# Language-model block: earlier slots for tile 0's layer norm and for the first weight splits

## The reference, cut to what matters

```
h = rms_norm(rms_norm(emb[ids]) @ proj.T)
h = h + attention(layernorm(h)) @ wo      # 32 query heads, 8 key/value heads of 16, causal softmax
h = h + (silu(n @ w_gate.T) * (n @ w_up.T)) @ w_down.T     with n = layernorm(h), 2048 hidden
layernorm(x) = (x - mean(x)) / sqrt(var(x) + 1e-5)
```

## Time and profile before

| | |
|---|---|
| median of three runs | 723.34 us (723.07 to 725.62) |
| profiled execution | 722.81 us, span 721.0 us |
| TensorE busy | 693.3 us (96%) |
| VectorE busy | 414.4 us (57%) |
| ScalarE busy | 334.5 us (46%) |
| GpSimd busy | 295.6 us (41%) |
| mean granted TensorE clock | 0.986 of full |

### The profile page before, as it was taken

The page is one execution under the profiler, slowest core; times in us unless marked ns, Lnnn a source line. Parts: engine busy times, 40 slices in busy tenths (PEclk is TensorE's granted clock), DMA queues, the critical chain, the costliest instruction groups (busy, mean ns, idle before and its releaser), DMA issues.

```text
span 721.0 us, 16350 instructions
## 1 busy us (share of the span) xinstructions
PE 693.3 (96%) x6399; PEld 530.2 (74%) x6399; DVE 414.4 (57%) x1041; ACT 334.5 (46%) x691; POOL 295.6 (41%) x398
## 2 busy tenths in 40 slices
PE   8459989999999999999999999999999999999998
PEld 5359679974898569965997489856996499847873
DVE  7867789885654556554655465555655365543320
ACT  6426368862565226631665046622674066512320
POOL 5020212241365426752565436642665246611220
PEclk9859999999999999999999999999999999999999
DMA  8759410011000110002000210012000300000000
GB/s 319 306 196 401 150 40 2 2 28 63 33 2 1 61 61 2 2 17 97 9 2 2 69 54 3 1 47 76 2 2 1 107 15 2 1 16 15 2 1 29
DMA packets 10459, 40.37 MB, mean 56 GB/s; under 512 B 1808, under 2 KB 2576, under 8 KB 8592
## 3 DMA queue, kind: packets, MB, share of 16 engines
q1 hardware_dynamic: 6912, 25.44, 9.1%
q0 software_dynamic: 3328, 13.11, 5.7%
q10 hardware_dynamic: 144, 0.79, 0.3%
HBM read 29.89 MB, written 9.44 MB: 55 GB/s over the span
## 4 chain that ended last, share of the span: by engine, by line
PE 88%; DVE 8%; ACT 2%; issue 1%; POOL 1%; DVEq 0%; POOLq 0%; ACTq 0%
PE banks L1106 15%; PE banks L1108 15%; PE banks L1107 15%; PE banks L1197 6%; PE banks L1199 6%; PE banks L1198 6%; PE banks L1060 4%; PE banks L1078 3%; PE banks L1049 2%; PE banks L1142 2%; PE banks L1144 2%; PE banks L1143 2%; PE banks L1084 1%; PE banks L1038 1%; PE banks L1085 1%
## 5 line engine op out<-in xcount | busy, mean ns | idle before, releaser
L1108 PE MATMUL banks<-xnT_and_h,ffn_weights 128*128 128x256 f16 x1024 | 279.0, 272 | 0.0
L1106 PE MATMUL banks<-xnT_and_h,ffn_weights 128*128 128x256 f16 x1024 | 278.8, 272 | 0.1
L1107 PE MATMUL banks<-xnT_and_h,ffn_weights 128*128 128x256 f16 x1024 | 278.9, 272 | 0.0
L374 POOL TENSOR_TENSOR gated_split<-gate_work,gated_split 128x256 f16<-128x256 f32 x128 | 86.7, 678 | 260.6 <-ACT gated_split L518 260.6
L378 POOL TENSOR_TENSOR weights_split<-weights,weights_split 128x512 f16<-128x512 f32 x96 | 111.3, 1159 | 0.0
L1106 PEld LDWEIGHTS banks<-xnT_and_h,ffn_weights 128*128 128x128 f16 x1024 | 101.0, 99 | 11.9 <-DVE xnT_and_h L878 0.6
L1108 PEld LDWEIGHTS banks<-xnT_and_h,ffn_weights 128*128 128x128 f16 x1024 | 100.0, 98 | 11.8
L1107 PEld LDWEIGHTS banks<-xnT_and_h,ffn_weights 128*128 128x128 f16 x1024 | 99.9, 98 | 11.2
L506 ACT ACTIVATE gate_work<-banks,scales 128x256 f32<-128x256 f32 x128 | 60.7, 474 | 99.8 <-PE banks L1108 99.7
L828 DVE SCALAR_TENSOR_TENSOR weights<-weights,counts_T 128x512 f32<-128x512 f32 x128 | 87.8, 686 | 11.6 <-ACT weights L514 11.5
L514 ACT ACTIVATE weights<-banks,scales 128x512 f32<-128x512 f32 x128 | 87.3, 682 | 14.5 <-PE banks L1060 14.5
(11 more groups left out here) (232 smaller groups left out, 1063.9 us busy)
## 6 DMA issues: line engine op xcount, KB each, us to landing
ffn_weights<-in_ffn_w SPq DMA_DIRECT2D x12, 1024.0 KB, 11.2
out_rows_dram<-ffn_weights SPq DMA_DIRECT2D x16, 256.0 KB, 2.0
xnT_and_h<-in_wqkv SPq DMA_DIRECT2D x1, 1536.0 KB, 8.6
local_table<-gated_split SPq DMA_DIRECT2D x2, 640.0 KB, 4.4
local_table<-xnT_and_h SPq DMA_DIRECT2D x2, 640.0 KB, 6.0
gated_split<-in_projT SPq DMA_DIRECT2D x4, 256.0 KB, 4.0
ffn_weights<-in_wo SPq DMA_DIRECT2D x1, 1024.0 KB, 10.6
token_table<-weights_split ACTq DMA_DIRECT2D x1, 768.0 KB, 5.2
```

Of the source, the lines that this page charges most:

```text
L374: g.tensor_tensor(gtl[:, j, :], g2[j % 2], gth[:, j, :], ALU.subtract).then_inc(gt_lo, 1)
L1106: t.matmul(o, wh, xTh[m % 2][:, c, :], start=c == 0, stop=False)
L1107: t.matmul(o, wh, xTl[m % 2][:, c, :], start=False, stop=False)
L1108: last = t.matmul(o, wl, xTh[m % 2][:, c, :], start=False, stop=c == DC - 1)
```

## The change

Only three tables change; no instruction is added or removed. In phase 0, steps of tile 0 go to earlier slots, as do the fetch for tile 2 and the splits of the first chunks. Four chunks were split by the end of phase 0, and then there are five. In phase 1 each chunk from 5 on is split one slot earlier than before. Steps of tile 1 stay where they are.

```diff
-FIRST_SLOTS = dict(yt=(11, 18), wo=(13, 19), ln=(16, 20), rs=(17, 20), xhat=(19, 20), xn=(20, 21), xl=(21, 21), fetch=(17, 20), m=(22, 3))
+FIRST_SLOTS = dict(yt=(11, 18), wo=(13, 19), ln=(14, 20), rs=(16, 20), xhat=(17, 20), xn=(19, 21), xl=(20, 21), fetch=(15, 20), m=(22, 3))
-HI_FIRST = {16: 0, 17: 1, 20: 2, 21: 3}
-LOW_FIRST = {19: (0,), 21: (1,), 22: (2,), 23: (3,)}
-HI_NEXT = {i - 4: i for i in range(4, NCH)}
+HI_FIRST = {16: 0, 17: 1, 18: 2, 20: 3, 21: 4}
+LOW_FIRST = {17: (0,), 19: (1,), 20: (2,), 22: (3,), 23: (4,)}
+HI_NEXT = {i - 5: i for i in range(5, NCH)}
```

## The result

Ten executions of each kernel: 726.16 us median after the change (725.14 to 729.36) against 724.59 before (723.07 to 725.62); the ratio is 1.0031, with a 95% interval of 1.002 to 1.0041. By the ratio that is 2.2 us more, by the medians 1.6. The profiled execution has a span of 723.4 us (721.0 before) and a time of 725.14.

The account below looks back on a forecast made before the run. Tile 1's chain was taken to set the gate/up start, with TensorE's own work behind it. Parts 1 and 2 gave 1.2 us, sum and fillers 0.7 to 0.8: +2.0 on 723.34, so 725.3, range 723.9 to 727.3.

Parts of the forecast that it names:

- The rest is TensorE's own work: Behind about 97.7 us TensorE runs its own order, so the end moves exactly as the first gate/up start does.
- Part 1: Slots 14 to 17: ln(0) and rs(0) move ahead of pair 7 on VectorE; its end comes 1.13 us later.
- Part 2: Slot 17: xhat(0) and chunk 0's split stand ahead of slot 18's subtraction, which starts 1.23 us later.
- the other branch of that working: The subtraction starting by ScalarE's copy, at 83.97; the forecast had VectorE's queue end last, at 84.35.
- Part 3: Slot 20: chunk 2's split delays the diagonal; sum and fillers add 0.7 to 0.8 us, gate/up +2.0 in all.
- Part 4 and 5: ScalarE's splits and chunks five ahead: priced 0, bounds 0 and +0.3; earlier fetches on GpSimd: nothing.
- Sum: Whole kernel: +2.0 us on the median 723.34 of the runs gives 725.3.
- likeliest range: Whole kernel, the likeliest case's own range: +1.3 to +2.6 us, 724.6 to 725.9.
- The clock rival: Clock falls on the thin stretch ahead of gate/up, 90.7 to 94 us: 727.3 us; chance 0.10.
- The price of 2.0: Clock fall's cost at 90.7 to 94 us: upper end of 1.2 to 2.0 us, taken for 727.3.
- the forecast place: The stretch from 90.7 to 94 us, ahead of gate/up, where a clock fall was placed.
- none of them is longer than 1.5 us: Argument against a clock fall: new TensorE idle times are short; the earlier fall came in a stretch without matmuls.

Follow-up runs that it names:

- norm_only: Kernel before with only tile 0's ln and rs moved, to slots 14 and 16; median 725.28 us against 724.36, ratio 1.0015.
- diag_first: Changed kernel with the down gram's diagonal ahead of chunk 2's split in slot 20; median 725.58 us against 724.36 of the kernel before, ratio 1.0015.
- again3: Changed kernel measured again without any edit, in a later group; median 725.99 us, ratio 1.0027 to the kernel before.
- again: Changed kernel measured once more without any edit; median 727.76 us, ratio 1.0051 to the kernel before.
- splits_only: Kernel before with only the three split tables as changed; median 726.28 us against 724.36, ratio 1.0029.
- rs_behind: Kernel before with tile 0's rs in slot 19, chunk 0's split halved, chunks 2, 3 high later, slots 14, 15 fillers removed; 724.73 us against 722.55, ratio 1.0012.

## Why the prediction was right, point by point

- **The rest is TensorE's own work.** Right: the end less the gate/up start is 628.0 us in both kernels, and 628.0 to 628.1 in every variant whose clock was full from gate/up on.
- **Part 1, the ready mark +1.13.** Measured +1.12, on the common scale, with the idle time of "over 1 us" at 1.03.
- **Part 2, chunk 0 ahead of the subtraction, +1.23 in all.** Measured 13.17 - 11.99 = 1.18 at the output product; xhat(1) 1.19. norm_only confirms the other branch of that working: without the split the chain goes by ScalarE's copy, +0.88.
- **Part 3, the diagonal, sum and fillers.** Forecast 0.7 to 0.8, measured 3.53 - 2.68 = 0.85, and 0.80 of it is back in diag_first. The sum waited 0.86 for L745, as said.
- **Part 4 and 5, nothing.** Right as far as the rest of 628.0 us and the unchanged wait row show; the fetches were not tested alone.
- **Sum.** +2.0 forecast; +2.04 measured between the fixed point and gate/up, and 2.2 by the ratio, 1.6 by the medians. That the chain came out within 0.04 is luck in part: Part 2 was 0.05 too high and Part 3 about 0.1 too low. The time itself, 726.16, lies 0.9 above the forecast of 725.3 and outside the likeliest range that ended at 725.9. That is the base and not the change: the forecast stood on a median of three executions, 723.34, and ten gave 724.59.
- **The clock rival was under-priced in chance and misplaced in part.** I gave it 0.10 and only one place. By the mean clock it came in 12 of 32 executions, in the changed kernel's profiles once at the forecast place (again3) and once behind the idle time ahead of tile 1's transposes (again). The price of 2.0 was too high for a fall at the first place, 1.29, and near for one at the second, 1.32 to gate/up and 1.7 with its first matmuls. The argument that failed is "none of them is longer than 1.5 us": in again a fall followed 1.03 us. The length of one idle time isn't the measure at all, as splits_only kept its clock over 1.85 us and rs_behind lost it over none. A forecast for the median had little need of the rival in the first ten, where six executions had no 0.981, but in again it set the median. That the first ten were not like again's five is luck.

## What to carry to other kernels

In a program written out per engine, list the links of the chain that ends last and ask of every step that moves whether it lands ahead of one of them on its engine. A step with a nearly free place (here rs(0), beside transposes and a copy) loses it when it goes earlier, and so does an order inside a slot that nobody meant (the diagonal behind a split). Differences of a few tenths are best compared from a fixed point behind the noise of the start.

## What the runs showed of the hardware that was not expected

- The granted clock differs between executions in places that no change touched. In the front it was 0.50 until about 50.5 us in the profile before, 53.1 in again and 55.2 in again3, and the fixed point moves with it: 71.88, 72.74 and 74.45 us.
- A half-clock stretch in the middle of a program came behind idle times of only 1.03 us (again) and 1.41 and 0.87 us (again3), and in rs_behind behind no idle time at all. In splits_only it didn't come behind 1.85 us. Such a stretch cost 1.3 us in again and 1.7 in again3, where the chain ran through it. In the profile's busy share the stretch ahead of the fall of rs_behind is 2.00 of 2.00 us, so a full busy row doesn't say that the clock is safe; the granted clock's column does.
